# Adjacency-weighted mean with residual and layer norm: tile 1 split like the rest, odd tiles normalised on GpSimd, new orders

## The reference

```python
mask = adj > 0
head = mask / max(sqrt(sum(mask * mask, axis=-1)), 1e-12)   # 1/sqrt(count) where adj > 0
inc = adj + head
e = (inc @ x) / sum(inc, axis=-1)
out = layernorm(x + e)          # over the 256 columns, eps 1e-5, no weights
```

## Time and profile before

| what | value |
| --- | --- |
| median of three runs | 413.19 us (411.52 to 413.34) |
| the profiled execution, its own time | 410.89 us |
| its span, first to last instruction | 409.1 us |
| granted TensorE clock | 1.000 |
| TensorE busy | 389.3 us, 95% |
| ScalarE busy | 371.4 us, 91% |
| VectorE busy | 364.2 us, 89% |
| GpSimd busy | 346.3 us, 85% |
| moved by DMA | 80.00 MB, mean 196 GB/s |

### The profile page before, as it was taken

One profiled execution on the slowest core, in us unless ns is written; L12 is line 12 of the kernel. 1 busy time (PEld: TensorE's weight loads), 2 busy tenths in 40 slices (PEclk: granted clock), 3 DMA queues, 4 the chain that ended last, 5 costly groups with the idle time before them and its releaser, 6 DMA issues.

```text
span 409.1 us, 8775 instructions
## 1 busy us (share of the span) xinstructions
PE 389.3 (95%) x2224; PEld 343.1 (84%) x2224; DVE 364.2 (89%) x757; ACT 371.4 (91%) x507; POOL 346.3 (85%) x222
## 2 busy tenths in 40 slices
PE   1689999999999999999999999999999999999995
PEld 0668889988888878888888888888888888888884
DVE  0897999999999999999999999999999999999932
ACT  4967999999999999999999999999999999998530
POOL 3111599999999999999999999999999999999970
PEclk9999999999999999999999999999999999999999
DMA  8999997576677667667666665767666666670020
GB/s 237 269 253 253 264 261 215 168 238 204 200 221 222 190 187 215 190 206 222 200 208 205 195 205 191 208 216 214 197 210 201 196 206 192 215 218 27 27 64 13
DMA packets 36183, 80.00 MB, mean 196 GB/s; under 512 B 9536, under 2 KB 17728, under 8 KB 36160
## 3 DMA queue, kind: packets, MB, share of 16 engines
q1 hardware_dynamic: 35776, 78.68, 66.1%
q10 hardware_dynamic: 384, 1.05, 0.8%
HBM read 75.50 MB, written 4.19 MB: 195 GB/s over the span
## 4 chain that ended last, share of the span: by engine, by line
PE 83%; POOL 4%; issue 4%; SPq 4%; DMA 3%; DVE 1%; ACT 1%; POOLq 0%; ACTq 0%
PE edge L1307 46%; PE edge L1321 23%; PE edge L1258 12%; POOL inc_split L564 3%; DMA x_stage<-in_x_dram 3%; SPq L156 3%; PE sums L1253 1%; SPq L179 1%; DVE incT L767 1%; POOL inc_split L578 0%; PE sums L1232 0%; SPq L184 0%; POOL small L548 0%; DVE inc L751 0%; ACT scaled L251 0%
## 5 line engine op out<-in xcount | busy, mean ns | idle before, releaser
L564 POOL TENSOR_TENSOR inc_split<-incT,inc_split 128x960 fp32r<-128x960 f32 x120 | 269.4, 2272 | 2.4 <-ACT inc_split L262 0.5
L1307 PE MATMUL edge<-x_split,inc_split 128*128 128x512 f32 (+1 forms) x930 | 223.4, 392 | 0.1
L1307 PEld LDWEIGHTS edge<-x_split,inc_split 128*128 128x128 f32 x930 | 168.1, 188 | 32.8 <-ACT inc_split L262 0.9
L751 DVE SCALAR_TENSOR_TENSOR inc<-raw,scaled 128x1024 f32<-128x1024 f32 x128 | 154.3, 1206 | 3.3 <-ACT scaled L251 2.4
L767 DVE STREAM_TRANSPOSE incT<-inc 128x1024 f32<-128x1024 f32 x128 | 156.3, 1230 | 0.7 <-PE edge L1258 0.4
L251 ACT ACTIVATE scaled<-raw,small 128x1024 f32<-128x1024 f32 x128 | 141.1, 1107 | 2.8 <-DVE inc L751 1.2
L240 ACT ACTIVATE sign_out<-raw 128x1024 int8<-128x1024 f32 x128 | 133.7, 1045 | 4.5 <-DMA raw<-in_adj_dram 4.3
L1321 PEld LDWEIGHTS edge<-x_split,inc_split 128*128 128x128 f32 x900 | 112.2, 191 | 2.3
L1321 PE MATMUL edge<-x_split,inc_split 128*128 128x256 f32 x900 | 113.5, 283 | 0.0
L262 ACT CAST inc_split<-incT 128x960 fp32r<-128x960 f32 x90 | 86.5, 984 | 0.7 <-DVE incT L767 0.7
L583 POOL TENSOR_TENSOR small<-small 128x1 f32<-128x1 f32 x24 | 13.2, 554 | 37.2 <-DVE small L733 37.0
(11 more groups left out here) (42 smaller groups left out, 138.8 us busy)
## 6 DMA issues: line engine op xcount, KB each, us to landing
raw<-in_adj_dram SPq DMA_DIRECT2D x504, 128.0 KB, 2.5
rows<-in_x_dram SPq DMA_DIRECT2D x32, 128.0 KB, 2.1
out_dram<-rows SPq DMA_DIRECT2D x32, 128.0 KB, 1.7
x_stage<-in_x_dram SPq DMA_DIRECT2D x12, 256.0 KB, 9.4
raw<-in_adj_dram ACTq DMA_DIRECT2D x8, 128.0 KB, 5.1
x_stage<-in_x_dram SPq DMA_DIRECT2D x4, 192.0 KB, 13.6
x_native<-in_x_dram SPq DMA_DIRECT2D x4, 64.0 KB, 5.7
```

The costliest lines, as they stand in the source:

```text
L564: nc.gpsimd.tensor_tensor(lo_of(s, q), incT[:, s, 0:SPLIT, q, :], hi_of(s, q).bitcast(fp32), ALU.subtract).then_inc(lo_by_pool, 1)
L751: nc.vector.scalar_tensor_tensor(inc[:, q, :], raw[:, s, q, :], 0.0, scaled[q % 2][:, :], ALU.is_gt, ALU.add, accum_out=part_sums[:, s, 0, ...
L1307: last = nc.tensor.matmul(edge[s][:, c0:c1], inc_split[s][:, 0, b, :, :].rearrange("p q j -> p (q j)"), x_split[:, b, :, :].rearrange("p h ...
```

## The change

- `FIRST_SPLIT` becomes 1: tile 0 alone is multiplied unsplit, tile 1 has native, rounded and remainder products. TensorE interleaves them: tile 0's first 15 chunks, tile 1's native ones, two chunks of tile 0, tile 1's rounded chunks 0 to 10 (each piece of x waits for its own split), the rest of tile 0, the rest of tile 1. ScalarE gets three more rounds, GpSimd one round and four remainders.
- `x_stage` now lies in the memory of `inc_split0`, so tile 2's rounds are the staged ones, and wait for tile 0.
- `normalise_odd` on GpSimd (tiles 1 to 29) and `normalise_even` on ScalarE (0 to 30) replace the other two; stores wait for one of two semaphores. `shift_of` is left for even tiles.
- The orders of all engines but SP are new, and written out up to tile 17; the loop goes from tile 18 to 27.

```diff
-        inc_split0 = sb("inc_split0", [P, 2, SPLIT, G, SQ], fp32r)
+        inc_split1 = sb("inc_split1", [P, 2, SPLIT, G, SQ], fp32r)
         with nc.sbuf_tensor("x_stage", [P, SPLIT, D], fp32) as x_stage:
             pass
-        inc_split1 = sb("inc_split1", [P, 2, SPLIT, G, SQ], fp32r)
+        inc_split0 = sb("inc_split0", [P, 2, SPLIT, G, SQ], fp32r)
...
-        FIRST_SPLIT = 2
+        FIRST_SPLIT = 1
...
-                sp.wait_ge(result_ready, t + 1)
+                sp.wait_ge(result_by_pool if s else result_by_act, t + 2 - s)
...
             # ScalarE, start
+            round_quarter(1, 1, 0, reuse=False)
+            split_x_hi(0)
             scale_early(1, 3)
-            split_x_hi(0)
+            split_x_hi(1)
+            round_quarter(1, 1, 2, reuse=False)
             sign_early(2, 0)
-            split_x_hi(1)
+            round_quarter(1, 1, 3, reuse=False)
...
-            round_quarter(2, 0, 2, reuse=False)
+            round_quarter(2, 0, 2, staged=True)
+            sign_early(3, 2)
             scale_early(3, 0)
-            sign_early(3, 2)
-            round_quarter(2, 0, 3, reuse=False)
             sign_early(3, 3)
+            round_quarter(2, 0, 3, staged=True)
...
             sign_quarter(12, 0, 6, 0)
-            sign_quarter(12, 0, 6, 1)
+            round_quarter(10, 0, 0)
             scale_quarter(11, 1, 0)
             round_quarter(10, 0, 2)
-            normalise(7, 1)
+            sign_quarter(12, 0, 6, 1)
             round_quarter(10, 0, 3)
...
             # ScalarE, end of the loop's body
-                sign_quarter(2 * u + 3, 1, u + 1, 1)
                 scale_quarter(2 * u + 2, 0, 1)
-                normalise(2 * u - 2, 0)
                 round_quarter(2 * u + 1, 1, 2)
                 round_quarter(2 * u + 1, 1, 3)
+                sign_quarter(2 * u + 3, 1, u + 1, 1)
+                normalise_even(2 * u - 2, 0)
...
             # GpSimd
+            def normalise_odd(t, s, alone=0, own=True):
+                if alone:
+                    pool.wait_ge(rstd_ready, alone)
+                elif own:
+                    pool.wait_ge(norm_ready, t + 5 - EARLY)
+                nc.gpsimd.tensor_scalar(y[:, s, :], y[:, s, :], mean_var[:, s, 0:1], norm_rstd[:, s, G:G + 1],
+                                        ALU.subtract, ALU.mult).then_inc(result_by_pool, 2)
...
+            low_quarter(1, 1, 0, reuse=False)
+            round_quarter(1, 1, 1, reuse=False)
+            low_quarter(1, 1, 1, reuse=False)
             norm_early(2, 0)
+            low_quarter(1, 1, 2, reuse=False)
             norm_early(2, 1)
             norm_early(2, 2)
+            low_quarter(1, 1, 3, reuse=False)
             norm_early(2, 3)
...
                 round_quarter(2 * u, 0, 1, own=False)
-                low_quarter(2 * u, 0, 1)
+                low_quarter(2 * u, 0, 1, rstd_of_tile=2 * u - 3)
+                normalise_odd(2 * u - 3, 1, own=False)
                 low_quarter(2 * u, 0, 2)
...
             rstd_of(30, 0)
+            normalise_odd(29, 1, alone=4)
             rstd_of(31, 1)
...
             # TensorE, start
+            unsplit_chunks(0, 0, 0, 15, {1: lambda: sum_early(1, 3), 6: lambda: sum_degree(0, 0)})
+            native_products(1, 1, {})
+            unsplit_chunks(0, 0, 15, 17)
+            sum_early(2, 0)
+            rounded_chunks(1, 1, 0, 11, {("hi", 9): lambda: sum_early(2, 1)}, first=True)
+            unsplit_chunks(0, 0, 17, B)
+            rounded_chunks(1, 1, 11, 30, {("hi", 12): lambda: sum_early(2, 2), ("hi", 24): lambda: sum_early(2, 3)},
+                                          first=True)
+            sum_early(3, 0)
+            remainder_chunks(1, 1, 0, 30, {("lo", 13): lambda: sum_early(3, 1), ("lo", 18): lambda: sum_degree(1, 1),
+                                           ("lo", 21): lambda: sum_early(3, 2)})
```

More of the change, by code:

```diff
@@ L400, in _ @@
             scale_quarter(10, 0, 0)
+            normalise_even(6, 0)
             scale_quarter(10, 0, 1)
-            normalise(6, 0)
             round_quarter(9, 1, 2)
@@ L616, in _ @@
             low_quarter(3, 1, 3)
+            rstd_of(1, 1)
+            norm_early(5, 0)
+            normalise_odd(1, 1, alone=2)
             round_quarter(4, 0, 1)
-            norm_early(5, 0)
             norm_early(5, 1)
-            rstd_of(1, 1)
             low_quarter(4, 0, 0)
@@ L656, in _ @@
             low_quarter(9, 1, 3)
+            norm_of(11, 1)
             round_quarter(10, 0, 1)
-            norm_of(11, 1)
             low_quarter(10, 0, 0)
+            normalise_odd(7, 1)
             low_quarter(10, 0, 1)
@@ L680, in _ @@
             low_quarter(13, 1, 3)
-            with pool.Fori(7, PAIRS - 2) as u:
+            norm_of(15, 1)
+            round_quarter(14, 0, 1)
+            low_quarter(14, 0, 0)
+            normalise_odd(11, 1)
+            low_quarter(14, 0, 1)
+            low_quarter(14, 0, 2)
+            low_quarter(14, 0, 3)
+            norm_of(16, 0)
+            round_quarter(15, 1, 1)
+            low_quarter(15, 1, 0)
+            low_quarter(15, 1, 1)
+            low_quarter(15, 1, 2)
+            low_quarter(15, 1, 3)
+            norm_of(17, 1)
+            low_quarter(16, 0, 0)
+            round_quarter(16, 0, 1)
+            normalise_odd(13, 1)
+            low_quarter(16, 0, 1)
+            low_quarter(16, 0, 2)
+            low_quarter(16, 0, 3)
+            norm_of(18, 0)
+            round_quarter(17, 1, 1)
+            low_quarter(17, 1, 0)
+            low_quarter(17, 1, 1)
+            low_quarter(17, 1, 2)
+            low_quarter(17, 1, 3)
+            with pool.Fori(9, PAIRS - 2) as u:
                 norm_of(2 * u + 1, 1)
@@ new lines, in _ @@
+            degree(12, 0)
+            transpose_quarter(14, 0, 1)
+            inverse_degree(12, 0)
+            y_first(12, 0, 6)
+            count_of(15, 1)
+            y_second(12, 0)
+            inc_quarter(14, 0, 2)
+            statistics(12, 0)
+            inc_quarter(14, 0, 3)
+            transpose_quarter(14, 0, 2)
+            mean_variance(12, 0)
+            transpose_quarter(14, 0, 3)
+            variance_eps(12, 0)
+            degree(13, 1)
+            inc_quarter(15, 1, 0)
@@ new lines, in _ @@
+            variance_eps(13, 1)
+            degree(14, 0)
+            inc_quarter(16, 0, 1)
+            inverse_degree(14, 0)
+            transpose_quarter(16, 0, 0)
+            y_first(14, 0, 7)
+            y_second(14, 0)
+            statistics(14, 0)
+            inc_quarter(16, 0, 2)
+            count_of(17, 1)
+            transpose_quarter(16, 0, 1)
+            inc_quarter(16, 0, 3)
+            transpose_quarter(16, 0, 2)
+            mean_variance(14, 0)
+            inc_quarter(17, 1, 0)
@@ new lines, in _ @@
+            variance_eps(14, 0)
+            transpose_quarter(16, 0, 3)
+            transpose_quarter(17, 1, 0)
+            inc_quarter(17, 1, 1)
+            degree(15, 1)
+            inverse_degree(15, 1)
+            inc_quarter(17, 1, 2)
+            y_first(15, 1, 7)
+            y_second(15, 1)
+            statistics(15, 1)
+            count_of(18, 0)
+            transpose_quarter(17, 1, 1)
+            mean_variance(15, 1)
+            transpose_quarter(17, 1, 2)
+            variance_eps(15, 1)
@@ L1103, in _ @@
+            shift_of(14, 0)
+            inc_quarter(17, 1, 3)
+            transpose_quarter(17, 1, 3)
+            with dve.Fori(9, PAIRS - 2) as u:
                 inc_quarter(2 * u, 0, 0)
@@ L1317, in split_products @@
                     lo_out = edge[1 - s][:, 0:D]
-                for b in range(SPLIT):
+                for b in range(b0, b1):
                     if ("lo", b) in middle:
```

564 lines of the change are left out of this document (305 added, 259 removed).

## The result

The changed kernel takes 423.14 us (median of 4 runs, 422.0 to 423.94), against 412.51 us for the kernel before beside it (411.52 to 413.34): a ratio of 1.0257, 95% interval 1.022 to 1.0294. The forecast was 412.1 us with a range from 409.2 to 414.8. It is slower by 10.6 us, well outside the range and above the slower rival's 416.8.

The account below looks back on a forecast made before the run. TensorE was taken to bound the kernel, with ScalarE the chain at the start and a load wait in the middle. Start +0.3, middle -1.4 and orders and store 0 gave -1.1 us: 412.1 us, range 409.2 to 414.8.

Parts of the forecast that it names:

- Normalise on GpSimd: Odd tiles' normalise moved to GpSimd: 0.35 us a pass, hidden in 0.64 us idle a pair; upper bound 1.18.
- The odd store: Odd tiles' store in the loop: at most 2 us later, 1 us to spare before a sign needs the load.
- The even store: Loop's late normalise_even: ScalarE waits 0.7 us a pair for loads behind its store; lead covers it, 0, bounds 0 and +1.0.
- Rival three: Pairs of tiles 6 to 31: GpSimd becomes the bound, +3.6 us, 416.8 us; chance 0.12.
- the prediction's own sign: Test in the loop: the prediction is wrong if the loop's tile isn't 11.55 us.
- The middle: Tiles 9 to 14: three quarters of 1.86 us lost to a late adj load saved, -1.4 us, bounds 0 and -1.86.
- The start: Up to tile 4: ScalarE's round (2, 3) holds TensorE, tile 1's 2.6 us hidden; +0.3 us, tile 4 at about 79.3.
- End: Last tile's products, statistics and store don't change: 0.

Follow-up runs that it names:

- the short pass: The changed kernel with GpSimd's normalise_odd given two immediates and a multiply for the subtraction, odd tiles left unnormalised: 416.0 us, ratio 1.0091.
- the store behind the loads: The changed kernel with every store, with its wait, issued behind the loads of the next tile's first quarter: 419.35 us, ratio 1.0177.

## Why the prediction was wrong

**Normalise on GpSimd (0.35 us, hidden): this step failed, and most of the loss hangs on it.** It measures 1.235 us, 0.88 more, above the upper bound of 1.18. With the short pass the ratio to the kernel before falls from 1.0257 to 1.0091. The bounds came from rows of passes over whole tiles (1.05 ns an element with one input) and of small ones; none of them reads its two factors per row. With immediates the pass takes 0.411 us, about what was forecast; the step priced the wrong form. But a right price would not have saved the forecast: with 0.411 us the kernel takes 416.0 us, still 4.2 above the kernel before and out of the range. The rest lies in the steps below.

The Trainium skill's "GPSIMD Engine Reference", section "4.1 Engine selection", was weighed in the prediction for 2 times VectorE, an estimate of 0.83 us. The measured 1.235 us is 3.0 times the 0.414 that VectorE took for one such pass alone, so the page's direction was right here. Whether it counts a pass over one tile with two factors per row as one input or two it doesn't say, and 3.0 is above either. With immediates, at 0.411, its "roughly line-rate" for one input agrees. The four other such passes on VectorE took 0.836 on average.

**The odd store ("at most 2 us later, 1 us to spare, together with the previous bound": nothing of its own): failed.** In the loop its result ends 13.3 us after the preceding tile's native products start (332.95 to 346.23), against 9.9 for ScalarE's before (277.14 to 287.04): 3.4 us later. Its store holds the loads behind it; moving that normalise alone gives back 0.77 us a pair. The prediction had seen the queue, but priced only the even side of it.

**The even store (0.7 us a pair of waiting, taken as 0, bounds 0 and +1.0): right in mechanism, the term too small.** With the short pass and the odd result early, a sign waits 0.84 us a pair behind the even store alone. The lead that the prediction counted on was there: in that kernel the first two pairs take 23.09 us, then come 23.31, 23.63 and 23.49, against its 23.3. Over the five pairs it lost 1.15 us, just above the upper bound and not 0.

**The two failed steps work together, through one wait.** With the even result early, 0.82 us more of GpSimd's pass make the odd result and its store later by as much, and the wait behind it goes from 0.72 to 1.77 us a pair; ScalarE's spare 0.51 is used up by the first part of it. So the loss in the last three pairs is 1.21 us with both faults, against 0.49 for the long pass with the loads out of the way and 0.41 for the late stores with the short pass.

The chain that ended last agrees. In the changed kernel's last three pairs it runs through normalise, store, x rows, the load of adj and ScalarE:

```profile
296.45 1.24 POOL rows L636
297.86 0.37 SPq L177
298.48 0.35 SPq L173
300.65 2.68 DMA raw<-in_adj_dram
```

GpSimd's remainders (L613), its main work, have 3% of that stretch. With the store behind the loads they alone have 52% of the same pairs; with the short pass and that store the chain of the loop is TensorE's.

Rival three (slower, GpSimd becomes the bound) was thus right for part of the kernel. Its formula would give 0.595 us a pair (1.235 - 0.64) and 13 x 0.595 - 0.7 + 0.3 = +7.3 us for the whole. In the written-out tiles the remainders have 45% of the chain from 120.25 us to tile 18. In the loop a bound of GpSimd's is there, 0.49 us a pair when the queue is out of the way, but in the changed kernel it isn't the one that holds: GpSimd has 0.89 us of idle time a pair, and before it had 0.85. By the prediction's own sign (the loop's tile isn't 11.55 us: it is 12.06) it is wrong.

**The middle (-1.4 us): failed.** Tiles 9 to 14 took 71.17 us before by their starts and 72.07 after; with the short pass 71.16. The wait for a load came back in other places. Of the 4.6 us from tile 4 to tile 18, 2.8 go with the length of the pass. Of the other 1.8, tiles 4 to 8 have 1.6 (59.40 us with the short pass, 57.79 before), where the kernel before lost nothing. With the short pass TensorE waits in tiles 7, 8 and 12, each time for ScalarE's rounding, after a sign had waited for a load in the tile before (tiles 6, 7 and 11); in the kernel before no matmul waits for a rounding there. The totals with the short pass:

```profile
ACT sign_out L242 <- DMA raw<-in_adj_dram: 4.0, 5, 1.2
...
PE edge L1454 <- ACT inc_split L264: 1.9, 3, 0.9
```

So the queue is the likely cause here too, but it isn't shown: moving the store brought a wait of VectorE in its place, no run took both away, and what the new orders of these tiles cost by themselves was not tried alone.

**The start (+0.3, tile 4 at 79.3): right, though the profile shows +1.2 and tile 4 at 80.13.** As forecast, the rounding of tile 2's last quarter holds TensorE and the 2.6 us taken off tile 1 are hidden:

```profile
44.89 1.06 ACT L242 ACTIVATE sign_out<-raw 128x1024 int8<-128x1024 f32 x1 [1.50 <-DMA raw<-in_adj_dram]
...
55.02 0.98 ACT L264 CAST inc_split<-incT 128x960 fp32r<-128x960 f32 x1
...
56.05 0.38 PE L1380 MATMUL sums<-small,quad_sum 128*128 128x1 f32 x2 [0.53 <-ACT inc_split L264]
56.29 0.95 PE L1454 MATMUL edge<-x_split,inc_split 128*128 128x256 f32 x4
```

The sign that waits for tile 2's last load began at 44.89, before the change at 43.69: the 1.2 us are this landing. It moves from run to run by as much: 42.92 to 45.95 us over five profiles with the old start, 43.18 to 45.83 over fourteen with the new one. From that sign to tile 4 the new start takes 35.21 to 35.25 us in twelve of them (the other two: 35.51, and 35.90 with the earliest landing); the old one 35.90 with the earliest landing, 35.22 in the profile before, and 34.6 to 34.8 in the three with the latest. So the new start costs 0 in the profiled pair and 0.4 to 0.6 us when the load comes late, around the +0.3.

**End (0): right**, +0.2.

## What to carry to other kernels

A pass that moves to another engine is priced in its own form: where no row has its operands, its bounds are not bounds, and one run of that operation by itself is worth more than ratios of other passes. On a queue that issues in order, a store that waits for a result holds every load behind it, so a normalise off the critical path sets when the next tile's data come; ask for each result that gets later what stands behind its store. A share of busy time doesn't name the bound: GpSimd was 96% busy in the loop before and after. The waits of the engine without spare time do, less what it was relieved of: ScalarE's, less 0.51 us a pair, gave every loop of the table to within 0.22 us.

## What the runs showed of the hardware

On GpSimd a 128x256 fp32 pass with two scalars took 0.411 us with immediates and multiplies, and 1.235 us with a subtraction and a multiplication by operands read per row, 4.8 ns against 1.6 ns an element of a row. Which of the two, operands or subtraction, makes the difference was not tried by itself. The landing of a load while the start's loads fill the queue varied by 3 us between profiles of kernels with the same start, which is more than most edits to that start could bring.
